# The bank copies of the output projection before the next block's transposes: one block of emission moved in an attention and FFN kernel

## The reference

```
x = x + layernorm(attn(layernorm(x)))       # sliding window 256, 16 heads of 64
x = x + layernorm(ffn(layernorm(x)))

attn: q, k, v = x @ w.T; per block of 256 queries, the keys are those of
      this block and of the one before, masked to a band of 256;
      softmax(q k / 8) v, then @ wo.T
ffn:  real = x @ cos(theta + theta_noise)
      imag = x @ sin(phi + phi_noise)
      sqrt(real*real + imag*imag)
```

## Time and profile before

| | us |
|---|---|
| median of 3 runs | 3954.79 (3954.76 to 3961.19) |
| the profiled execution, own time | 3953.05 |
| its span, slowest core (core 3) | 3951.5 |
| spans of the eight cores | 3933.0 to 3951.5 |
| PE busy | 3174.4 (80% of the span) |
| DVE busy | 1658.1 (42%) |
| ACT busy | 1368.5 (35%) |

### The profile page before, as it was taken

How to read it: one execution, slowest core, us unless ns; L and a number is a source line. 1 busy time by engine, 2 the same in 40 slices (tenths; PEclk the granted TensorE clock), 3 DMA queues, 4 the chain that set the end, 5 groups by cost and what they waited for, 6 DMA issues and landing times.

```text
span 3951.5 us, 51977 instructions; the slowest of 8 cores (3933.0 to 3951.5 us)
## 1 busy us (share of the span) xinstructions
PE 3174.4 (80%) x19808; PEld 2103.0 (53%) x19808; DVE 1658.1 (42%) x3600; ACT 1368.5 (35%) x2176; POOL 111.7 (3%) x215
## 2 busy tenths in 40 slices
PE   0019988989888898988889897988889898888984
PEld 0016555556555556656555555655555565556552
DVE  2323436172543616263352617254361725436162
ACT  3433333242433424242342325243332424234241
POOL 1100000000000000000000000000000000000000
PEclk9997898989898998989899798989999898989987
DMA  6773231414233150423315141422314142331503
GB/s 208 259 259 151 97 159 65 184 51 171 107 120 138 63 211 24 171 107 128 149 57 200 65 173 62 171 107 107 150 65 193 43 171 107 128 138 56 213 12 138
DMA packets 54162, 511.25 MB, mean 129 GB/s; under 512 B 5792, under 2 KB 5920, under 8 KB 28576
## 3 DMA queue, kind: packets, MB, share of 16 engines
q0 software_dynamic: 30384, 266.35, 16.8%
q1 hardware_dynamic: 23536, 241.58, 16.7%
HBM read 465.97 MB, written 41.94 MB: 129 GB/s over the span
## 4 chain that ended last, share of the span: by engine, by line
PE 68%; DVE 20%; issue 5%; DMA 4%; ACT 3%; DVEq 0%; POOL 0%; ACTq 0%; SPq 0%; POOLq 0%
PE pb L516 34%; PE pb L461 18%; DVE attn_sb L700 5%; PE pb L669 5%; DVE stats L697 5%; PE pb L769 4%; DVE ao_sb L807 3%; PE pb L659 2%; PE pb L731 2%; DMA wsc<-pl 2%; PE pb L401 1%; DVE attnT_sb L742 1%; DVE sc L841 1%; DVE sc L927 1%; PE pb L352 1%
## 5 line engine op out<-in xcount | busy, mean ns | idle before, releaser
L697 DVE TENSOR_REDUCE stats<-pb 128x1 f32<-128x384 f32 (+2 forms) x512 | 269.3, 526 | 811.1 <-PE pb L669 811.1
L769 PE MATMUL pb<-v_sb,attnT_sb 128*128 128x64 f32 x2880 | 473.5, 307 | 91.1 <-DVE attnT_sb L742 89.7
L769 PEld LDWEIGHTS pb<-v_sb,attnT_sb 128*128 128x128 f32 x2880 | 431.6, 223 | 165.4 <-issue 162.5
L711 ACT ACT_TABLE_LOAD x256 | 328.4, 1283 | 516.1 <-DVE attn_sb L700 515.8
L461 PE MATMUL pb<-fmh,slot0h 128*128 128x256 bf16 x1024 | 280.4, 274 | 262.4 <-DMA slot0l<-wsc 262.4
L516 PE MATMUL pb<-slot2h,fmh 128*128 128x512 bf16 x992 | 375.9, 379 | 13.4 <-ACT ao_sb L898 13.4
L516 PE MATMUL pb<-slot2h,fml 128*128 128x512 bf16 x992 | 375.9, 379 | 0.0
L516 PE MATMUL pb<-slot2l,fmh 128*128 128x512 bf16 x992 | 375.9, 379 | 0.0
L461 PE MATMUL pb<-fmh,slot1h 128*128 128x256 bf16 x960 | 273.2, 285 | 88.5 <-DVE sc L841 88.5
L700 DVE TENSOR_SCALAR attn_sb<-pb,stats 128x384 f32<-128x384 f32 (+2 forms) x512 | 303.5, 593 | 56.4 <-DVE stats L697 1.8
L414 ACT ACT_TABLE_LOAD x32 | 41.1, 1283 | 785.9 <-PE pb L401 785.9
(11 more groups left out here) (114 smaller groups left out, 4707.0 us busy)
## 6 DMA issues: line engine op xcount, KB each, us to landing
slot0h<-wsc SPq DMA_DIRECT2D x33, 2048.0 KB, 10.4
slot1h<-wsc SPq DMA_DIRECT2D x33, 2048.0 KB, 10.5
slot0l<-wsc POOLq DMA_DIRECT2D x33, 2048.0 KB, 12.6
slot1l<-wsc POOLq DMA_DIRECT2D x33, 2048.0 KB, 12.5
slot2h<-wsc SPq DMA_DIRECT2D x33, 2048.0 KB, 10.4
slot2l<-wsc POOLq DMA_DIRECT2D x33, 2048.0 KB, 12.4
x_sb<-x POOLq DMA_DIRECT2D x32, 512.0 KB, 6.2
y<-sc POOLq DMA_DIRECT2D x32, 512.0 KB, 3.4
```

The lines of the kernel that those rows point to most:

```text
L697: ev[f"mx_{g}_{uu}"] = ve.inc(vector.reduce_max(stats[:, P + up:P + up + 1], kept, axis=AX.X))
L711: ev[f"ex_{g}_{uu}"] = ac.inc(scalar.activation(attn_sb[:, up * SL:up * SL + (c1 - c0 + 1) * 128], attn_sb[:, up * SL:up * SL + (c1 - c0 + ...
L769: ins = tensor.matmul(pb[b_av][:, (h % 8) * DH:(h % 8 + 1) * DH], lhsT, rhs, start=(first_in_bank and ci == 0), stop=(last_in_bank and ci ...
```

## The change

The call that emits the next block's transposes is moved behind the copies of the four banks and their guard. No instruction is added, removed or resized. On TensorE and ScalarE the order stays what it was, since the moved copies are VectorE's alone. On VectorE the four L841 copies of `op_g` now stand in front of the four L424 instructions of the next block instead of behind them.

```diff
@@ -830,9 +830,6 @@
                          srch=fmh2, srcl=fml2)
             pump_loads(o_use + 4)
 
-            if not last:
-                emit_n1t(g + 1)
-
             @block.vector
             def _(vector):
                 ins = None
@@ -842,6 +839,9 @@
                         sc2[:, ti * 512:(ti + 1) * 512], pb[ti][:])
                 ev[f"oev_{g}"] = ve.inc(ins)
             kb.bank_set([0, 1, 2, 3], [(ve, ev[f"oev_{g}"])])
+
+            if not last:
+                emit_n1t(g + 1)
 
             def _sc2_ap(tt, half):
                 return sc2[:, tt * 1024 + half * 512:tt * 1024 + (half + 1) * 512]
```

## The result

| | before | after |
|---|---|---|
| median, us | 3955.74 (10 runs) | 3865.52 (10 runs) |
| ratio to before, 95% interval | | 0.9765 (0.9755 to 0.9775) |
| profiled execution, its span | 3953.05, 3951.5 | 3867.2, 3865.7 |

The change makes the kernel 2.35% faster; 3866 was forecast. The experiments ran on four chips, each with executions of the kernel before beside them; its fastest took 3953.7 us in the runs of the table and 3954.3 to 3959.0 us on those chips, so that times of different chips can be compared to about 5 us.

The account below looks back on a forecast made before the run. TensorE, busy 80% of the span, was taken as the bound. Gap 4.27 plus clock 1.6 gave 5.87 us per block, times 15 = 88 us off 3953.05; with the median's 1.7 us offset, 3866 was predicted, range 3846 to 3889.

Parts of the forecast that it names:

- Where the wait was: Before the k projection: TensorE waits for bank 0's guard, set by the last copy; 88.5 us in 15 waits.
- The copies, hidden: On VectorE: the four moved copies, 2.47 us, are covered by the output projection and the 16 transposes.
- The gap: Before the k projection: the wait falls from 5.90 to 1.63 us, 4.27 us per block.
- the rival in which L424 holds it anyway: Before the k projection: L424's last part holds it, so at most 36 us gained, 3917; chance 0.02.
- The clock in the gap: K projection: the clock stays at 1.00, so it takes 21.12 us, a gain of 1.6 us per block.
- The rival of the lost clock: K projection: the clock falls anyway and only the gap's 64 us are gained, 3889; chance 0.07.
- No new wait behind: Before the v projection: ScalarE's k copies come in time, with 3.1 us of room; opposing rival 3909, chance 0.03.
- Slower: Attention and projections around it: more lower-clock time; 16 us more per block would give 3985; chance 0.02.
- The attention stage, taken as zero: Attention stages: lengths 82.40 or 84.80 us could shift the total about 17 us either way; taken as zero.
- One of the prediction's own signs of being wrong: Attention stages: the prediction is wrong if they lengthen by more than they vary today, 2.4 us.

Follow-up runs that it names:

- experiment 3: Kernel before, old order, but each of the four banks guarded by its own copy instead of the last one: 3958.3 us, ratio 0.9974.
- experiment 1: Changed kernel, but the k projection's first tile also waits for the second layernorm's statistics (L297): 3960.4 us, ratio 0.9997.
- Experiment 2: Changed kernel with the k projection held for the second layernorm's statistics and 26 constant matmuls filling the gap: 3955.0 us, ratio 0.9974.
- Experiment 4: Kernel before, but the k projection goes through banks 4 to 7 first, then 0 to 3: 3981.7 us, ratio 1.0042.
- experiment 8: Changed kernel with ScalarE's function table loaded early and each of the four squares guarding its own bank: 3807.0 us, ratio 0.9615.
- experiment 7: Changed kernel with a tiny ScalarE Copy ahead of the split's waits, so the function table loads early: 3853.4 us, ratio 0.9713.
- experiment 9: Changed kernel with 28 constant matmuls added to each attention stage, four behind each of the first seven score pairs: 3817.3 us, ratio 0.9628.
- with 12 and with 17 matmuls: Changed kernel with 12 or 17 constant matmuls between the transposes and the k projection of each block: ratios 0.9817 and 0.9877.
- experiment 10: Changed kernel with early function table, a guard per bank for the squares and 28 matmuls in each attention stage: 3763.5 us, ratio 0.9500.
- experiment 5: Changed kernel with the transposes' emission moved one step further, behind the second layernorm: 4003.3 us, against 3954.3 to 3971.1 before.
- the version with 22 matmuls: Changed kernel with 22 constant matmuls between the transposes and the k projection of each block: ratio 0.9871.

## Why the prediction was right, step by step

*Where the wait was.* Right. The guard of bank 0 held the k projection: experiment 3 loosens that guard alone and takes 27 of the 88.5 us of waiting away, and experiment 1 puts another wait at the same place and restores the time before.

*The copies, hidden.* Right. The four copies were forecast to follow the layernorm and the ends of the tiles, and they do; the last one has 1.72 us to spare before L424, against the 1.7 of the prediction.

*The gap.* 4.27 us per block were forecast from the wait in front of the cos projection. Measured: (88.5 - 24.1) / 15 = 4.29. The k projection starts 0.84 us after the first low part (2881.36 to 2882.20), as the row of the cos projection had it, so the rival in which L424 holds it anyway (3917) is out.

*The clock in the gap.* Right. The k projection takes 21.12 us in every block, as was worked out from the q projection, and the stretch behind the gap reads 1.00. Over 15 blocks that is 24.0 us (340.8 to 316.8), and 15 x 1.6 = 24 were forecast. Experiment 2 parts the two terms: with the long gap but the clock kept up the k projection takes the same 21.12 us. The rival of the lost clock (3889) is out.

*No new wait behind.* Right. The v projection follows the k projection at once. ScalarE's first k copy ends at 2900.16, 3.16 us before the v projection starts, and 3.1 were forecast. Experiment 4 shows that the wait for ScalarE's k copies was a real danger, and what it costs.

*Slower.* The time at the lower clock did not grow: from the first L352 on it is 629 us on the slowest core before and 555 after. On all eight cores of both kernels every record of the clock reads 1.00 or 0.50, and none a level between. But this rival named the right place: the attention stage is where 1 to 3 us per block can go, for reasons that have nothing to do with its own work.

*The attention stage, taken as zero.* This term was the weak one. In the changed kernel it came out near zero: the 15 stages add up to 1237.0 us against 1234.7 before, so that the two other terms (64 us of gap, 24 us of clock) make up the 86 us between the spans. That was partly luck. In experiment 2 the same term was the whole saving, in experiment 3 it took 21 us and the k projection's clock 6 us of the 27, and in experiment 8 it went the other way by 37 us. The range did hold 17 us either way for it, worked out from two lengths, 82.40 and 84.80 us. Stages of 85.6 us were there already in the kernel before, on the cores 0, 1 and 5, and 85.5 us is the usual length in experiments 2 and 7. A truer range would have had its upper end some 10 us higher. One of the prediction's own signs of being wrong did show, a stage longer than any before: on the slowest core and four others the second stage takes 87.0 or 87.1 us. It is one of 15 and did not move the sum.

*What stays open.* That a higher clock in the stage makes it shorter is shown by experiment 9. That the period can settle is seen in the last blocks of nine versions: 228.6 to 228.8 us in experiment 2 and on cores 1 and 2 of experiment 4, 225.2 with 12 and with 17 matmuls, 221.8 in the changed kernel (cores 1 to 3) and in experiment 7, 218.4 or 218.5 in experiments 8 and 9, 214.8 in experiment 10, which are 3.3 to 3.7 us apart. Others do not settle so: the kernel before and experiment 1 alternate, with 226.7 to 227.0 and 230.2 to 230.7 us in most blocks, and experiments 3 and 5 and the version with 22 matmuls keep changing. That the steps come from the clock, which would change at moments of its own while the stage's length depends on where in it they fall, is argued and not shown. That 22 matmuls cost so little more than 17 lies in the attention stages, 18 us shorter in all; why they are shorter is open.

## What to carry to other kernels

A guard that is met by an instruction late in a queue costs the engine that waits for it, though the bank was free long before: put an instruction that only empties a finished bank ahead of those that wait for later work on the same queue. Moving the waiting instructions back further still, behind the layernorm, made this kernel slower than before. A gap of TensorE is worth more than its length if the clock falls in it, and a similar gap elsewhere in the same trace told here whether it would. In a loop whose stages run partly at the lower clock, don't take the sum of removed waits for the gain: read the period of a block in each version, and test whether keeping TensorE busy in its waiting stretches makes the stage shorter.

## What the runs showed of the hardware that was not expected

Matmuls whose result nobody uses can shorten a stage: 28 of them in each attention stage took the sum of the 15 stages from 1237.0 to 1191.9 us. Block periods gather at few values, near 214.8, 218.5, 221.8, 225.2 and 228.7 us, so that 1.1 us of work more per block left the period of the settled blocks as it was in one version, and 0.8 us less took about 3 us off it in another.
